# Running two pyramid levels later on TensorE, and pairing stores and loads on SyncE's queue

## Time and profile before

| | |
|---|---|
| median of 3 runs | 1411.79 us (1411.63 to 1413.0) |
| the profiled execution, its own time | 1411.72 us |
| span in its profile, first to last instruction | 1410.0 us |
| PE, ACT, DVE, POOL busy | 86%, 82%, 77%, 51% of the span |
| moved over the span | 381 GB/s |
| mean granted TensorE clock | 0.995 |

### The profile page before, as it was taken

The page is one execution under the profiler, slowest core; times in us unless marked ns, Lnnn a source line. Parts: engine busy times, 40 slices in busy tenths (PEclk is TensorE's granted clock), DMA queues, the critical chain, the costliest instruction groups (busy, mean ns, idle before and its releaser), DMA issues.

```text
span 1410.0 us, 18859 instructions
## 1 busy us (share of the span) xinstructions
PE 1206.1 (86%) x5632; PEld 711.5 (50%) x5632; DVE 1079.9 (77%) x1280; ACT 1153.0 (82%) x1282; POOL 712.4 (51%) x1316
## 2 busy tenths in 40 slices
PE   4888888888888888888888888888888888888886
PEld 2555445545554554455455545544554555455443
DVE  4677778787777777787877777787878777777874
ACT  4788888888888888888888888888888888888886
POOL 3455545544554554455445545544554555455443
PEclk9999999999999999999999999999999999999999
DMA  9899999999999999999999999999999999999966
GB/s 381 342 394 393 390 386 393 391 386 389 394 391 385 391 393 391 384 392 393 384 392 392 392 383 392 392 390 385 392 393 384 389 391 395 383 390 393 389 241 238
DMA packets 139281, 537.08 MB, mean 381 GB/s; under 512 B 8193, under 2 KB 8193, under 8 KB 139265
## 3 DMA queue, kind: packets, MB, share of 16 engines
q1 hardware_dynamic: 139264, 536.90, 99.2%
HBM read 268.44 MB, written 268.44 MB: 381 GB/s over the span
## 4 chain that ended last, share of the span: by engine, by line
PE 83%; ACT 7%; issue 6%; POOL 2%; DMA 1%; DVE 1%; POOLq 0%; ACTq 0%; SPq 0%
PE l_ps L381 11%; PE l_ps L356 9%; PE l_ps L382 8%; PE l_ps L383 8%; PE l_ps L363 8%; PE l_ps L355 8%; PE l_ps L359 8%; PE l_ps L361 8%; ACT l L443 6%; PE l_ps L391 4%; PE l_ps L392 2%; PE mean_ps L341 2%; PE l_ps L393 2%; POOL l L255 2%; PE mean_ps L342 2%
## 5 line engine op out<-in xcount | busy, mean ns | idle before, releaser
L431 ACT ACTIVATE squares<-xs,negm 128x4096 bf16<-128x4096 f32 x128 | 475.0, 3711 | 4.2
L255 POOL TENSOR_TENSOR l<-l,col_fix 128x4 f32<-128x4 f32 x128 | 27.8, 217 | 603.6 <-ACT l L443 603.6
L305 DVE SCALAR_TENSOR_TENSOR h<-xs 128x2048 f32<-128x2048 f32 x128 | 291.6, 2278 | 8.5 <-DMA xs<-x_dram 8.5
L311 DVE SCALAR_TENSOR_TENSOR h<-xs,h 128x2040 f32<-128x2040 f32 x128 | 291.0, 2274 | 0.0
L222 POOL TENSOR_TENSOR newt<-r 128x1 f32<-128x1 f32 x128 | 270.3, 2112 | 37.9 <-DVE ve L273 37.9
L470 ACT ACTIVATE xs<-xs,negmr,r_plus 128x2048 f32<-128x2048 f32 x128 | 269.2, 2103 | 0.0
L381 PE MATMUL l_ps<-l,w_first 128*128 128x256 f32 x256 | 92.6, 442 | 179.9 <-POOL l L255 179.9
L458 ACT ACTIVATE l<-l_ps 128x256 f32<-128x256 f32 x128 | 49.0, 383 | 169.1 <-PE l_ps L383 169.1
L272 DVE RECIPROCAL r<-std 128x1 f32<-128x1 f32 x128 | 21.1, 165 | 213.5 <-ACT std L451 213.5
L283 DVE SCALAR_TENSOR_TENSOR xs<-l,r,xs 128x512 f32<-128x512 f32 x128 | 99.1, 774 | 80.2 <-POOL r L230 80.2
L317 DVE SCALAR_TENSOR_TENSOR a<-h 128x1024 f32<-128x1024 f32 x128 | 156.9, 1225 | 4.4
(11 more groups left out here) (83 smaller groups left out, 2445.2 us busy)
## 6 DMA issues: line engine op xcount, KB each, us to landing
xs<-x_dram SPq DMA_DIRECT2D x256, 1024.0 KB, 10.7
y_dram<-xs SPq DMA_DIRECT2D x256, 1024.0 KB, 6.1
```

The lines of the kernel that those rows point to most:

```text
L305: nc.vector.scalar_tensor_tensor(h1[:, b], v[:, :, 0:W:2], 2.0, v[:, :, 1:W:2], ALU.mult, ALU.add).then_inc(h1_part, 1)
L311: nc.vector.scalar_tensor_tensor(h1[:, b, :, 1:W1], v[:, :, 1:W - 2:2], 1.0, h1[:, b, :, 1:W1], ALU.mult, ALU.add, accum_out=hsum[:, b:b + ...
L431: nc.scalar.activation(squares[:], xs[:, u % SLOTS, :], ACT.Square, bias=negm[:, b:b + 1], accum_out=sumsq[:, b:b + 1]).then_inc(sumsq_rea ...
```

## The change

TensorE runs `level2` one step later and `level3` two steps behind. `finish` of VectorE is split: the corner of group u-2 is added first, then level 1 of group u-1. On ScalarE `scale_beside(u-1)` moves from before `evacuate1(u)` to behind `root(u)`, and `evacuate2` now works on group u-1. The tail has two steps. SyncE issues the stores of groups n and n+1 and then the loads of groups n+6 and n+7, for even n. GpSimd's program is unchanged but for the second tail step, in which it has nothing to do.

```diff
-AHEAD = 7
+LAG_L3 = 2
+AHEAD = 6
...
-        TAIL = [(LAPS, u) for u in range(LAG)]
+        TAIL = [(LAPS, u) for u in range(LAG_L3)]
...
-            for lap in range(LAPS):
-                for k in range(SLOTS):
-                    step(lap, k, last=lap == LAPS - 1)
+            for n in range(0, G, 2):
+                for k in (n, n + 1):
+                    store(k // SLOTS, k % SLOTS)
+                for k in (n + AHEAD, n + AHEAD + 1):
+                    if SLOTS <= k < G:
+                        load(k // SLOTS, k % SLOTS)
...
+                if exists(base, u - LAG_L3):
+                    add_corner(base, u - LAG_L3)
                 if exists(base, k):
-                    finish(base, k)
+                    add_level1(base, k)
...
                 if exists(base, u):
                     mean(base, u)
-                if exists(base, u - LAG):
-                    level3(base, u - LAG)
+                if exists(base, u - LAG_L3):
+                    level3(base, u - LAG_L3)
                 if exists(base, u):
                     level1(base, u)
                     variance(base, u)
-                    level2(base, u)
+                if exists(base, u - LAG):
+                    level2(base, u - LAG)
...
                 if make:
                     moments(base, u)
-                if done:
-                    scale_beside(base, u - LAG)
-                if make:
                     evacuate1(base, u)
                     root(base, u)
                 if done:
+                    scale_beside(base, u - LAG)
                     scale_bottom(base, u - LAG)
-                if make:
-                    evacuate2(base, u)
+                    evacuate2(base, u - LAG)
```

More of the change, by code:

```diff
@@ L273, in rstd, with add_level1 @@
                 nc.vector.tensor_scalar(ve[:, d], var_ps[:, d], EPS, None, ALU.add).then_inc(r0_ready, 1)
-            def finish(base, k):
+            def add_level1(base, k):
                 b = k % 2
@@ L285, in finish, with add_corner @@
                                                ALU.add).then_inc(l1_added, 1)
+            def add_corner(base, k):
+                b = k % 2
+                d = slice(b, b + 1)
+                img = rows(k % SLOTS)[:, 0:TOP].rearrange("p (c s) w -> p c s w", s=RPP)
                 dve.wait_ge(l3_ps_ready, base + k + 1)
-                img = top.rearrange("p (c s) w -> p c s w", s=RPP)
                 for s in range(RPP):
```

## The result

The changed kernel takes 1377.43 us (median of 4 runs, 1376.94 to 1379.86) where the kernel before takes 1411.71 in the same comparison: ratio 0.976, 95% interval 0.9743 to 0.9777. The forecast was 1380. The profiled execution took 1377.11 us.

What follows compares the result with a forecast made beforehand. An engine loop of 10.77 us per step, not the 99.2% busy DMA, was taken as the bound. 1411.7 - 29.6 (steps) - 3.4 (head) + 1.5 (tail) = 1380.2 us; range 1374 to 1386 for this case, 1359 to 1403 with rivals.

Steps and rivals of the forecast that it cites:

- The pace setter: Steady step of the kernel before: a serial engine loop of 10.77 us sets the pace; the DMA only just keeps up.
- TensorE's order: Level 2 on the group before loses its 1.39 us wait and starts at about E+0.2 (E: first evacuation's start).
- ScalarE's order: Second evacuation now queues behind both scalings; level 3 waits 0.15 us, step 10.53 us, gain 29.6 us.
- The rival of 10.36: Level 3 does not wait; the VectorE loop alone sets a 10.36 us step, 1359 us in all; chance 0.13.
- VectorE: The corner waits some 0.8 us for level 3, covered by the existing 1.67 us square-root wait; cost 0.
- SyncE's order: Paired stores and loads need 20.76 us of DMA per pair, hidden by 0.3 us under the loop's 21.06.
- the two changes belong together: Engine order needs the paired transfers: in SyncE's old order a pair would take 21.50 us of DMA, over 21.06.
- My price of 0.62 to 0.85 us per turn: DMA time lost at each rate dip, 2 us at 289 or 240 GB/s instead of 419; 0.74 taken.
- the second dip: DMA rate dip, once per step before; pairing was to leave one per pair of steps where there were two.
- Look-ahead: SyncE's loads: one load less of look-ahead costs nothing, 13 us of lead; loads 8 and 9 leave near 74 us.
- Head: First steps: TensorE's idle stretch and 2.7 us half-clock loss move one step ahead; 3.4 us gained, bounds 0.8 to 6.1.
- Tail: End of the run: the last three top and bottom stores queue behind group 126's late corner; cost 1.5 us.

Runs made afterwards that it cites:

- e2: The kernel before with only SyncE's order changed to pairs of stores and loads, six ahead: 1411.5 us, ratio 0.9995.
- e5: The changed kernel, pairs kept, with the right part's scaling back before the first evacuation and VectorE's reciprocal moved behind the row sum: 1311.83 us, ratio 0.9293.
- e3: The changed kernel with one ScalarE edit undone, the right part's scaling back in front of the first evacuation: 1358.37 us, ratio 0.9623.
- e1: The changed kernel with SyncE's old order, one group's stores, then one group's loads, seven ahead: 1378.18 us, ratio 0.9757.
- d1: Transfers alone, no engine computing: each group loaded and stored unchanged, one group's stores then one group's loads, six ahead: 1285.29 us.
- e7: The kernel before with only VectorE's reciprocal moved behind the row sum: 1649.73 us, ratio 1.1685.
- e8: The changed kernel with one more ScalarE operation, a copy of 1024 elements per partition, ahead of each second evacuation: 1636.83 us, ratio 1.1589.
- e6: The changed kernel with the right part's scaling before the first evacuation, VectorE's reciprocal behind the row sum, and SyncE's old order: 1311.53 us, ratio 0.9291.
- e4: The changed kernel with VectorE's reciprocal moved behind the row sum: 1370.18 us, ratio 0.9699.

## Why the prediction was right, and where it was not

**The pace setter** was named rightly: an engine loop, not the DMA (e2: no change from SyncE's order; e5: 100 us below the kernel before with the same bytes). One piece of my evidence was misread. L158, on which SyncE waited twice for stores, is not the wait in front of a reload, as I had it; that one is L142. L158 stands at the end of SyncE's program and waits for the last stores. So no reload waited for a store at all, which speaks for the engine loop even more.

**TensorE's order.** Level 2 starts without a wait, at E+0.14 (E+0.2 forecast). Right.

**ScalarE's order.** The forecast step was 4.88 + 5.65 = 10.53 us; measured 4.85 + 5.66 = 10.51, and 10.506 as the mean. L464 came 0.03 us earlier, because the scaling L476 took 2.09 us and overlapped it by 0.10, where I had 2.10 and 0.08. Over 125 steps the 0.024 us are 3 us, nearly the whole error of the forecast. The rival of 10.36 is exactly what e3 measures, and the sign of the edit was right: moving the scaling behind the root costs time.

**VectorE.** Its new wait for the corner is 107.8 / 128 = 0.84 us (0.8 forecast), covered as forecast: it still waits 162.0 / 128 = 1.27 us per step for the square root.

**SyncE's order** is the step that failed. The failed statement is that the two changes belong together, since a pair in the old order would be 21.50 us of DMA. e1 runs that order at 21.01 us per pair without a wait for loads, d1 shows 19.93. My price of 0.62 to 0.85 us per turn was read correctly as a fall of the rate, but a fall of the rate in a queue that has time to spare was not a cost. All bytes at the rate of the windows next to the dip, 419 GB/s, would have been the better estimate: 20.02 us. The error did not move the forecast, since on either reading the DMA stayed hidden at 10.51; this part of the forecast came true on a wrong cost. Nor did the second dip go away with the second turn. Over 20 pairs of the kernel after (from 300 us on, in windows of 1 us, averaged by their place in the pair) the rate falls twice per pair, to 272 and to 333 GB/s, and with the old order, in e1, to 282 and 334. In e5, where VectorE waits for loads, no single window of 1 us from 300 to 420 us is under 410. And the DMA share stays at 1.00 to 1.03, not "under 100% with short gaps" as I had it:

```profile
700.00:705.00 5.00, 4.57 (x26) 2.60 (x28) 4.09 (x8) 4.86 (x5) 2.70 (x9) 1.00 1.02 419
707.00:712.00 5.00, 4.06 (x22) 3.18 (x22) 3.78 (x6) 4.90 (x8) 3.44 (x4) 1.00 1.00 342
712.00:716.00 4.00, 4.00 (x22) 1.81 (x22) 3.12 (x6) 3.88 (x3) 1.21 (x7) 1.00 1.03 417
```

The 358 GB/s per core that the prediction quotes from "HBM Reference" of the Trainium skill, section Specifications, is what that page gives each core when both cores of a pair stream; this program runs on one core, and d1 moved 421 GB/s.

**Look-ahead.** The first reload leaves at 73.54 us (74 forecast), and nothing waits for it.

**Head.** Forecast E(1) = 34.6, E(2) = 45.1, half clock from about 24 to 32 us; measured 34.50, 45.00, and the clock in TensorE's windows:

```profile
24.00:26.00 2.00, 0.00 (x0) 0.78 1.01 401
26.00:28.00 2.00, 1.57 (x7) 0.50 1.04 416
...
30.00:32.00 2.00, 2.00 (x6) 0.51 1.05 418
32.00:34.00 2.00, 2.00 (x10) 1.00 1.01 401
```

**Tail.** 1.5 us forecast, 1.1 measured, and the reason holds: the corner of group 126 is done at E+6.95 (E+7.1 forecast), and its top store and the two of group 127 leave only then, at 1365.39, 1366.22 and 1369.74.

## What to carry to other kernels

Write down each loop that closes from one step to the next with its length, not just the one on the critical chain: here they were 10.77 us (before), 10.51 (made by the change), 10.36 and 9.37, beside 9.96 us of transfers, and each edit is worth only the distance to the next. Opening the last two together gave 1311.83 us, 65.6 us below the changed kernel, where one alone gave 19 and the other 7. A busy DMA queue and a dip in its rate are no cost until a run with the transfers alone says what they take.

## What I had not expected of the hardware

- The granted clock makes a cliff. An idle stretch of 1.39 us in front of level 2 in each step left it at 1.00 from 100 to 1300 us; 2.17 us in e7, or twice 0.93 us close together in e8, came with 0.50 in about two steps of three, each of those 1.6 us longer. So e7 ran 17% slower than the kernel before, for a wait that grew by 0.78 us, and e8 19% slower than the changed kernel, for an operation of 0.94 us.
- The shares of the DMA engines read 1.02 while 389, 399, 414 and 421 GB/s were moved (before, after, e6, d1). The share does not tell how much room is left. Why the rate dips once per step in the less pressed kernels, with one turn per pair as with two, and not in e5 or with the transfers alone, was not settled.
- GpSimd's four-column fix takes 0.20 us (before), 0.98 (e7), 1.25 (median of e4) or 1.50 (one step of e5), depending on what VectorE runs beside it.
